# Stacking the halves of keys and queries by 96 transfers, not by TensorE

## The chip, the cores and the metric

The kernel runs on one NeuronCore of one Trainium2 chip. The metric is the device time of one execution in microseconds (us). The kernel before took 898.96 us, the median of three runs (898.91 to 900.83). The names of the engines: TensorE (PE, and PEld for its weight loads), VectorE (DVE), ScalarE (ACT), GpSimd (POOL) and SyncE (SP), which here only issues transfers.

## What is computed

A small vision tower of two layers over 32 images of 37 tokens (36 patches and a class token), 256 features wide: patch projection, a linear-recurrence attention, a quantized convolutional feed-forward, then a causal softmax attention and a mixture of 32 experts. The change lies in the second attention, of 16 heads of 16 features:

```python
q = jnp.einsum('bse,hde->bshd', x, Wq) + bq
k = jnp.einsum('bse,hde->bshd', x, Wk) + bk
v = jnp.einsum('bse,hde->bshd', x, Wv) + bv
mask = jnp.triu(jnp.full((s, s), -jnp.inf, dtype=x.dtype), k=1)
scores = (jnp.einsum('bqhd,bkhd->bhqk', q, k) + mask) * inv_scale
attn = jax.nn.softmax(scores, axis=-1)
out = jnp.einsum('bhqk,bkhd->bqhd', attn, v)
```

All is float32 in the reference. The kernel keeps each float32 operand of a product as two float16 halves, high and low, and multiplies high by high, high by low and low by high.

## The kernel before

Each engine has a program of its own, written out by hand; they meet at counting semaphores. `T` is 32 x 37 = 1,184 tokens, cut in `NCH` = 4 chunks of `CH` = 296. Features lie on the 128 partitions, in two groups `c` = 0, 1 of 128 features (8 heads each).

**Projection** (line 2037 on). TensorE computes for group 0 the keys (`i` = 1) and the queries (`i` = 0), chunk by chunk, then the values, then keys and queries of group 1. ScalarE writes the high half of each with its bias (L1252: `k1h`, `q1h`), VectorE the low half (L1692: `k1l`, `q1l`). The value halves (L1259, L1698) go to `vt`, and SyncE puts them on three groups of partition rows of `v3` by 18 transfers inside the core's memory (line 914 on; `load` is L887): three thirds, three residues of the sequence number, and 32 and 5 rows of each.

**Turning** (`turn_halves`, L2060 on). A score product contracts over 48 rows: 16 features of a head three times, as (high, high, low) of the queries against (high, low, high) of the keys. These rows must lie one above the other, and two heads lie in one stack, at rows 0 to 47 and 64 to 111. `PICK` says which half goes to which third. TensorE moves them there by products with 0/1 matrices (`picks`, made by GpSimd), 32 turns of four matmuls (L2069) of 296 columns, into two banks of its accumulator memory each; the turns go in turn to ScalarE (L488) and VectorE (L490), which copy 112 x 592 values to `qs` and `ks` as float16. 26 turns stand before the attention's loop, six in it, two in each of the first three units.

**Attention**, 16 units `k` of four sequences and eight heads; units 0 to 7 are group 0, 8 to 15 group 1. In program order TensorE issues in step `k`: the scores of unit `k` (L2085 puts the mask, L2094 the 32 score products), the turning of the probabilities of unit `k` - 3 (L2108), the mix of unit `k` - 4 (L2119 are four filling matmuls, L2127 the 32 products with `v3`). The first mix waits for the 18 transfers of `v3`. VectorE takes maximum and difference (L1706, L1710), ScalarE the exponential and the high half (L1273, L1277), GpSimd the low half (L1038), ScalarE and VectorE copy the turned probabilities (L1270, L1719), VectorE divides (L1724, L1725). In steps 7, 9, 11 and 13 ScalarE also makes the high half of an expert's weights, and in steps 9 and 11 VectorE a low half (L586); SyncE loads the next weights after each low half (L540). When the last unit is divided, the result is turned back (L2147), normalized and handed to the experts.

Of the kernel before, what the change touches and what calls it, by code (L numbers as in the profile page):

```python
# [13 lines left out]
DH = D // H  # L14
# [27 lines left out]
for _n, _w in [("cb", 6), ("cw", 24), ("gb", 2), ("dbb", 1), ("opb", 2), ("fcw", 24), ("fcb", 8), ("bq", 2),  # L42
# [32 lines left out]
    + ["pad1", "qk1h", "v1h", "v_one"]  # L75

    + ["v3", "turned", "turned_act", "turned_dve"]
# [136 lines left out]
TURNED = [(c, h, p, i) for c in range(2) for h in range(2) for p in range(4) for i in (1, 0)]  # L214
INSIDE = 6
FIRST_TURNS = len(TURNED) - INSIDE
TURN_LAG, MIX_LAG = 3, 4


def turner(t):  # L220
    return ("dve", "act")[(t // 2 + t) % 2]


def turn_bank(t):
    return 2 * (t % 4) if t < FIRST_TURNS else 4 + 2 * (t % 2)


def turn_holder(t):
    return max((x for x in range(t) if turn_bank(x) == turn_bank(t)), default=None)


def turned_inside(k):
    return range(FIRST_TURNS + 2 * k, FIRST_TURNS + 2 * k + 2) if 2 * k < INSIDE else ()


def turned_by(who, t):
    return sum(turner(x) == who for x in range(t + 1))
# [3 lines left out]
KK = 3 * DH  # L241

# [14 lines left out]
def tower(nc, a, out, probe=None):  # L257
    place = plan_tiles()
    order = list(place)
    with ExitStack() as ctx:  # L260
# [67 lines left out]
        def after(eng, key):  # L328

            eng.wait_ge(emptied[who(key)], nth(key))  # L330

        def cols(q, n=CH):
            return slice(q * n, (q + 1) * n)
# [108 lines left out]
        picks = carve(9344, 2, 2, 4, 64 + KK, dt=F16)  # L442
        v3 = carve(26272, B, H, DH + 1, dt=F16, parts=3 * S)
        o1 = carve(4608, BP, H, DH)
# [34 lines left out]

        def stack(eng, name, turns):  # L480
            for t in turns:
                c, h, p, i = TURNED[t]
                if turner(t) == name:
                    eng.wait_ge(ev["turned"], t + 1)
                    dst = (ks if i else qs)[:, 4 * c + p, 2 * CH * h:2 * CH * h + 2 * CH].rearrange("p (i t) -> p i t", i=2)
                    src = psum[0:64 + KK, turn_bank(t):turn_bank(t) + 2, 0:CH]
                    if name == "act":
                        eng.activation(dst, src, ACT.Copy).then_inc(ev["turned_act"], 1)  # L488
                    else:
                        eng.tensor_copy(dst, src).then_inc(ev["turned_dve"], 1)  # L490

        def stacked(eng, t):
            for name in ("act", "dve"):
                eng.wait_ge(ev["turned_" + name], turned_by(name, t))
# [390 lines left out]
        def _(sp):  # L885
            def load(dst, src, name):
                sp.dma_start(dst, src).then_inc(ev[name], 16)  # L887
# [23 lines left out]
            for e in range(2):  # L911
                load(wraw[:, e], a["wmoe"][0, e], f"wraw{e}")
            after(sp, ("v1", (VT + 1) // 2 - 1))
            for n, kind in enumerate((0, 1, 0)):
                for b in range(3):
                    m = (B - b + 2) // 3
                    for r, w in ((0, 32), (32, S - 32)):
                        load(v3[S * n + r:S * n + r + w, b:B:3].rearrange("p b h v -> p b (h v)"),
                             vt[S * b + r:S * b + r + w, kind, 0:m].rearrange("p n h v -> p n (h v)"), "v3")
            if not probe:  # L920
                moe_sp(sp)
# [7 lines left out]
        def _(pool):  # L929
# [96 lines left out]
            link(pool.memset(picks, 0.0))  # L1026
            for pattern in range(2):
                for n, kind in enumerate(PICK[pattern]):
                    for x in range(2):
                        ins = pool.tensor_copy(picks[:, pattern, kind, :, 64 * x + DH * n:64 * x + DH * n + DH],  # L1030
                                               identh[:].rearrange("p (i x d) -> p i x d", i=4, x=2)[:, :, x])
                        if (pattern, n, x) == (1, 2, 1):
                            ins.then_inc(ev["pad1"], 1)
                        else:
                            link(ins, hold=False)
# [7 lines left out]
        def _(act):  # L1043
# [218 lines left out]
            stack(act, "act", range(FIRST_TURNS))  # L1262
            for k in range(len(UNITS) + TURN_LAG):
                stack(act, "act", turned_inside(k))
                x = k - TURN_LAG
                if x >= 0:
                    act.wait_ge(ev["att_t"], 2 * x + 1)
                    if x >= 2:
                        act.wait_ge(ev["att_o"], x - 1)
                    act.activation(pt[0:3 * S, x % 2, 0:8], pt_bank(0), ACT.Copy).then_inc(ev["att_pa"], 1)  # L1270
                if k < len(UNITS):
                    act.wait_ge(ev["att_e"], k + 1)
                    act.activation(e_[0:101, k % 3], e_[0:101, k % 3], ACT.Exp, scale=DH ** -0.5).then_inc(ev["att_p"], 1)  # L1273
                    act.wait_ge(ev["att_p"], k + 1)
                    if k >= 3:
                        act.wait_ge(ev["att_t"], 2 * (k - 2))
# [10 lines left out]
        def _(dve):  # L1287
# [413 lines left out]
            stack(dve, "dve", range(FIRST_TURNS))  # L1701
            for k in range(len(UNITS) + MIX_LAG):
# [10 lines left out]
                stack(dve, "dve", turned_inside(k))  # L1713
# [39 lines left out]
        def _(pe):  # L1753
# [304 lines left out]
            halves = ((q1h, q1l), (k1h, k1l))  # L2058

            def turn_halves(t):  # L2060
                c, h, p, i = TURNED[t]
                if t == 0:
                    pe.wait_ge(ev["pad1"], 1)
                    after(pe, ("qk1", 0, 1, NCH - 1))
                if turn_holder(t) is not None:
                    stacked(pe, turn_holder(t))
                for x in range(2):
                    for kind in range(2):
                        ins = pe.matmul(psum[0:64 + KK, turn_bank(t) + x, 0:CH], picks[:, i, kind, p],  # L2069
                                        halves[i][kind][:, c, cols(2 * h + x)], start=kind == 0, stop=kind == 1)  # L2070
                ins.then_inc(ev["turned"], 1)

            for t in range(FIRST_TURNS):
                turn_halves(t)

            def scores(k):
                c, n = UNITS[k]
                if k < 2:
                    stacked(pe, max(t for t in range(FIRST_TURNS) if turn_bank(t) == 2 * k))
                elif n % 4 == 0:  # L2080
                    stacked(pe, 16 * c + 2 * n + 7)
# [17 lines left out]
            def turn_probs(k):  # L2099
                pe.wait_ge(ev["att_lo"], k + 1)  # L2100
                if k == 0:
                    stacked(pe, len(TURNED) - 1)
                else:
                    pe.wait_ge(ev["att_pa"], k)
                    pe.wait_ge(ev["att_pb"], k)
# [26 lines left out]
            for k in range(len(UNITS) + MIX_LAG):  # L2132
                if k < len(UNITS):
                    scores(k)
                for t in turned_inside(k):
                    turn_halves(t)
# [85 lines left out]
```

## Time and profile before

| | us |
|---|---|
| median of three runs | 898.96 |
| lowest and highest | 898.91, 900.83 |
| the profiled execution's own time | 899.29 |
| its span (first to last instruction) | 897.6 |
| TensorE busy | 762.5 |
| VectorE busy | 614.6 |
| ScalarE busy | 389.3 |
| GpSimd busy | 185.9 |

The profile is of one execution. Times of its rows count from the start of the span, so the execution's own time is the span and 1.7 us around it. An engine's busy time is the sum of its instructions; that of TensorE is modelled, since its matmuls overlap. "<-" in a row names what is written and what is read, with partitions x elements behind, and in brackets stands how long the engine had been idle and what ended it. Most of the kernel's data lies in one large buffer, `arena`, so many rows read "arena<-arena".

### The profile page before, as it was taken

How to read it: one execution, taken by the hardware profiler on the slowest of the kernel's cores; microseconds unless marked ns; L12 is line 12 of the kernel's file. 1: busy time of each engine (PE TensorE's matmuls, PEld its weight loads, DVE VectorE, ACT ScalarE, POOL GpSimd, SP SyncE). 2: the span in 40 equal slices, each digit the busy share in tenths (PEclk: the TensorE clock that was granted, in tenths of full speed). 3: DMA queues.
4: the chain of work that ended last, by engine and by line, in shares of the span. 5: the costliest groups of instructions: out<-in, count | busy, mean ns of one | idle time of the engine just before them, and what ended most of it. 6: DMA issues, size and time to landing. Idle time of an engine off the chain costs nothing.

```text
span 897.6 us, 19046 instructions
## 1 busy us (share of the span) xinstructions
PE 762.5 (85%) x7314; PEld 562.6 (63%) x7314; DVE 614.6 (68%) x974; ACT 389.3 (43%) x559; POOL 185.9 (21%) x197
## 2 busy tenths in 40 slices
PE   4786956989996966877598996699999999999997
PEld 3554735954543654656278884467777777777775
DVE  5796597658877476788767887757777755555554
ACT  5344653620224232765356983434444423333322
POOL 7000791005989801000300430000000000000000
PEclk9986877999999996987999998889999999999999
DMA  8000000020000000010112001044444312222221
GB/s 304 1 1 2 2 1 3 3 95 0 1 0 1 0 2 0 1 33 6 35 30 59 14 28 36 1 148 147 157 151 151 125 53 79 65 68 62 67 65 54
DMA packets 24070, 46.02 MB, mean 51 GB/s; under 512 B 2605, under 2 KB 10541, under 8 KB 23629
## 3 DMA queue, kind: packets, MB, share of 16 engines
q1 hardware_dynamic: 24013, 45.21, 16.5%
q8 instruction: 42, 0.69, 0.3%
q14 instruction: 15, 0.12, 0.0%
HBM read 41.91 MB, written 1.36 MB: 48 GB/s over the span
## 4 chain that ended last, share of the span: by engine, by line
PE 70%; DVE 18%; ACT 5%; issue 4%; POOL 1%; DMA 1%; SPq 0%; DVEq 0%; ACTq 0%; POOLq 0%
PE psum L1765 11%; PE psum L1766 11%; PE psum L1767 11%; PE psum L1941 6%; PE psum L1951 4%; PE psum L825 4%; PE psum L826 4%; PE psum L827 4%; PE psum L2069 1%; DVE arena L1445 1%; PE psum L1991 1%; PE psum L1922 1%; DVE arena L1638 1%; DVE arena L1310 1%; PE psum L2108 1%
## 5 line engine op out<-in xcount | busy, mean ns | idle before, releaser
L1765 PE MATMUL psum<-xh,arena 128*128 128x296 f16 (+1 forms) x664 | 196.4, 296 | 12.0 <-DVE xl L1318 6.3
L1766 PE MATMUL psum<-xl,arena 128*128 128x296 f16 (+1 forms) x664 | 196.3, 296 | 0.0
L1767 PE MATMUL psum<-xh,arena 128*128 128x296 f16 (+1 forms) x664 | 196.1, 295 | 0.0
L694 DVE TENSOR_TENSOR arena<-arena 128x592 f16<-128x592 f32 x68 | 52.7, 776 | 61.2 <-ACT arena L605 60.9
L600 ACT ACTIVATE arena<-psum 128x592 f32<-128x592 f32 x66 | 43.8, 664 | 115.3 <-PE psum L1767 115.3
L1765 PEld LDWEIGHTS psum<-xh,arena 128*128 (+2 forms) x664 | 66.2, 100 | 35.6 <-issue 9.4
L749 DVE TENSOR_TENSOR arena<-psum,arena 128x592 f32<-128x592 f32 x64 | 49.6, 775 | 50.9 <-PE psum L1767 50.2
L825 PE MATMUL psum<-arena 128*128 128x296 f16 x272 | 79.7, 293 | 4.6 <-DVE arena L694 3.8
L826 PE MATMUL psum<-arena 128*128 128x296 f16 x272 | 79.7, 293 | 0.0
L605 ACT ACTIVATE arena<-arena 128x592 f16<-128x592 f32 x66 | 46.0, 697 | 77.6 <-DVE arena L688 74.8
L827 PE MATMUL psum<-arena 128*128 128x296 f16 x272 | 79.6, 293 | 0.0
L1765 PE MATMUL psum<-arena 128*74 128x74 f16 (+3 forms) x348 | 59.2, 231 | 23.6 <-DVE arena L1328 12.7
L1767 PEld LDWEIGHTS psum<-xh,arena 128*128 (+2 forms) x664 | 66.3, 100 | 20.5
L1766 PEld LDWEIGHTS psum<-xl,arena 128*128 (+2 forms) x664 | 66.3, 100 | 19.6
L1941 PE MATMUL psum<-arena 128*128 128x512 f32 (+1 forms) x160 | 65.8, 550 | 14.3 <-DVE arena L524 14.3
L524 DVE TENSOR_TENSOR arena<-arena,psum 128x320 f32<-128x320 f32 (+7 forms) x67 | 54.1, 808 | 8.4 <-PE psum L1941 8.4
L1941 PEld LDWEIGHTS psum<-arena 128*128 128x128 f32 x160 | 30.3, 195 | 46.5 <-issue 28.4
L1007 POOL TENSOR_TENSOR arena<-arena 128x64 f32<-128x64 f32 (+23 forms) x24 | 43.7, 1819 | 75.8 <-ACT arena L1170 58.7
L1767 PE MATMUL psum<-arena 128*74 128x74 f16 (+3 forms) x348 | 59.2, 232 | 0.0
L1766 PE MATMUL psum<-arena 128*74 128x74 f16 (+3 forms) x348 | 59.2, 231 | 0.0
L688 DVE TENSOR_TENSOR arena<-arena 128x592 f32<-128x592 f32 x68 | 52.7, 776 | 8.8 <-ACT arena L600 1.9
L1765 PEld LDWEIGHTS psum<-arena 128*74 128x74 f16 (+2 forms) x348 | 38.8, 117 | 28.3 <-issue 24.6
(317 smaller groups left out, 1583.1 us busy)
## 6 DMA issues: line engine op xcount, KB each, us to landing
arena<-comb SPq DMA_DIRECT2D x62, 296.0 KB, 3.3
arena<-in_wmoe SPq DMA_DIRECT2D x34, 384.0 KB, 3.0
arena<-in_xt SPq DMA_DIRECT2D x4, 864.0 KB, 9.5
arena<-in_w SPq DMA_DIRECT2D x2, 1024.0 KB, 6.6
arena<-arena SPq DMA_DIRECT2D x6, 187.0 KB
arena<-in_ctrl SPq DMA_DIRECT2D x1, 1056.0 KB, 9.1
out<-arena SPq DMA_DIRECT2D x2, 512.0 KB, 3.1
arena<-in_wlin SPq DMA_DIRECT2D x1, 768.0 KB, 4.4
```

Of the source, the lines that this page charges most:

```text
L524: return eng.tensor_tensor(dst[:, 0:w * HJ * DH].rearrange("p (t j v) -> p t j v", j=HJ, v=DH), a_, u, ALU.mult)
L605: act.activation(ah[:, s_], t1, ACT.Copy).then_inc(ev["ah"], 1)
L688: dve.tensor_tensor(t1, t1, sg, ALU.mult).then_inc(ev["a"], 1)
L694: dve.tensor_tensor(al[:, s_], t1, ah[:, s_], ALU.subtract).then_inc(ev["al"], 1)
L749: dve.tensor_tensor(t1v, up, cb_[:, s_].rearrange("p (c t) -> p c t", c=2), ALU.mult).then_inc(ev["t1"], 1)
L825: pe.matmul(dst, high, ah[:, s_, cols(ch)], start=start, stop=False, skip_group_check=True)
L826: pe.matmul(dst, high, al[:, s_, cols(ch)], start=False, stop=False, skip_group_check=True)
L827: ins = pe.matmul(dst, low, ah[:, s_, cols(ch)], start=False, stop=stop, skip_group_check=True)
L1765: pe.matmul(dst, wh, mh, start=start, stop=False)
L1766: pe.matmul(dst, wh, ml, start=False, stop=False)
L1767: return pe.matmul(dst, wl, mh, start=False, stop=stop)
L1941: pe.matmul(row(g0, g1 - g0), negident, ring[:, n_ % RING, 64 * (g0 - base):64 * (g1 - base)], start=False, stop=s_ + 1 == g0, skip_group_ ...
```

## The change

The turning products and their copies are gone, with the 0/1 matrices and the functions that ordered them. SyncE issues a transfer for each head, group and third in their place: 8 heads x 3 thirds x (keys, queries) x 2 groups = 96, each of 16 partitions by 1,184 float16 values (2,368 bytes), from the place where the half was written to its rows of `qs` or `ks`. For each group and kind, 16 (the thirds with the high half) wait for ScalarE's four high halves, and 8 for VectorE's last low half. TensorE waits for 48 landed transfers before unit 0 and for the other 48 before unit 8. The buffer `o1` of the results is moved, since the halves are now read longer.

```diff
@@ SyncE's program
+            halves = ((q1h, q1l), (k1h, k1l))
+
+            def stack(c, i):
+                sp.wait_ge(ev["qk1h"], NCH * (2 * c + 2 - i))
+                for part in range(2):
+                    if part:
+                        after(sp, ("qk1", i, c, NCH - 1))
+                    for n, kind in enumerate(PICK[i]):
+                        for h in range(8 if kind == part else 0):
+                            row = 64 * (h % 2) + DH * n
+                            load((qs, ks)[i][row:row + DH, 4 * c + h // 2],
+                                 halves[i][kind][DH * h:DH * h + DH, c], f"stacked{c}")
+
+            stack(0, 1)
+            stack(0, 0)
             after(sp, ("v1", (VT + 1) // 2 - 1))
             for n, kind in enumerate((0, 1, 0)):
...
+            stack(1, 1)
+            stack(1, 0)
             if not probe:
                 moe_sp(sp)
@@ TensorE's program
-            for t in range(FIRST_TURNS):
-                turn_halves(t)
-
             def scores(k):
                 c, n = UNITS[k]
-                if k < 2:
-                    stacked(pe, max(t for t in range(FIRST_TURNS) if turn_bank(t) == 2 * k))
-                elif n % 4 == 0:
-                    stacked(pe, 16 * c + 2 * n + 7)
+                if n == 0:
+                    pe.wait_ge(ev[f"stacked{c}"], 16 * STACKS)
+                if k == 0:
+                    after(pe, ("qk1", 0, 1, NCH - 1))
...
                 pe.wait_ge(ev["att_lo"], k + 1)
-                if k == 0:
-                    stacked(pe, len(TURNED) - 1)
-                else:
+                if k:
                     pe.wait_ge(ev["att_pa"], k)
                     pe.wait_ge(ev["att_pb"], k)
...
-                for t in turned_inside(k):
-                    turn_halves(t)
@@ VectorE's program (ScalarE's alike)
-            stack(dve, "dve", range(FIRST_TURNS))
...
-                stack(dve, "dve", turned_inside(k))
@@ GpSimd's program
-            link(pool.memset(picks, 0.0))
-            for pattern in range(2):
...
@@ buffers
-        o1 = carve(4608, BP, H, DH)
+        o1 = carve(21536, BP, H, DH)
```

SyncE's queue before, from the first expert weights to the first transfers of the values and from their last to the next weights (L887 is `load`, in_wmoe are expert weights, arena<-arena is a transfer inside the core's memory; sizes are partitions x runs x values):

```order
L887 DMA arena<-in_wmoe 128x768 [waits emptied_f2]
L887 DMA arena<-in_wmoe 128x768
L887 DMA arena<-arena 32x11x272 [waits emptied_dve]
L887 DMA arena<-arena 5x11x272
...
L887 DMA arena<-arena 32x10x272
L887 DMA arena<-arena 5x10x272
L540 DMA arena<-in_wmoe 128x768 [waits wlo] x4
```

The same place with the change (`load` is now L848, the weights' L501):

```order
L848 DMA arena<-in_wmoe 128x768 [waits emptied_f2]
L848 DMA arena<-in_wmoe 128x768
L848 DMA arena<-arena 16x1184 [waits qk1h]
L848 DMA arena<-arena 16x1184 x15
L848 DMA arena<-arena 16x1184 [waits emptied_dve]
L848 DMA arena<-arena 16x1184 x7
...
L848 DMA arena<-arena 32x11x272 [waits emptied_dve]
L848 DMA arena<-arena 5x11x272
...
L848 DMA arena<-arena 16x1184 [waits emptied_dve]
L848 DMA arena<-arena 16x1184 x7
L501 DMA arena<-in_wmoe 128x768 [waits wlo] x4
```

48 of the new transfers stand ahead of the 18 of the values, and 48 behind them.

TensorE's queue before, between the last projection and the scores of unit 0 (L1767 is a projection product, L2069 a turning product, L2085 and L2094 the scores):

```order
L1767 MATMUL psum<-xh,arena 128x296
L2069 MATMUL psum<-arena 112x296 [waits emptied_dve,pad1]
L2069 MATMUL psum<-arena 112x296 x15
L2069 MATMUL psum<-arena 112x296 [waits turned_dve,turned_act]
L2069 MATMUL psum<-arena 112x296 x3
...
L2085 MATMUL psum<-arena 101x296 [waits turned_dve,turned_act]
L2085 MATMUL psum<-arena 101x296
L2094 MATMUL psum<-arena 64x37 x8
```

And with the change (L1731 the projection, L2031 and L2040 the scores, L2052 the turned probabilities, L2063 the filling of the first mix):

```order
L1731 MATMUL psum<-xh,arena 128x296
L2031 MATMUL psum<-arena 101x296 [waits emptied_dve,stacked0]
L2031 MATMUL psum<-arena 101x296
L2040 MATMUL psum<-arena 64x37 x8
...
L2052 MATMUL psum<-identh,arena 111x101 [waits att_pb,att_pa,att_lo]
L2052 MATMUL psum<-identh,arena 111x101 x15
L2063 MATMUL psum<-arena 101x222 [waits v3]
...
L2031 MATMUL psum<-arena 101x296 [waits att_e,stacked1]
```

The scores now follow the projection directly, with a wait on `stacked0`; a wait on `stacked1` stands before the scores of unit 8.

## Rows read from the trace of the kernel before

**Rows 1.** The page, busy time of each engine (share of the span) and instructions.
```profile
PE 762.5 (85%) x7314; PEld 562.6 (63%) x7314; DVE 614.6 (68%) x974; ACT 389.3 (43%) x559; POOL 185.9 (21%) x197
```

**Rows 2.** Chain of waits, 470 to 486 us: start, us, what.
```profile
470.64 0.54 DVE arena L1692
...
471.31 12.27 PE psum L2069 x96
...
483.61 1.47 DVE arena L490 x2
```

**Rows 3.** Instructions of the turning's lines: ns min/median/max, first and last start.
```profile
L2069 PE MATMUL psum<-arena x128: 289/289/333, 471.3 to 491.6; 128*112 128x296 f16 x128
...
L490 DVE CAST arena<-psum x16: 764/765/776, 472.0 to 492.0; 112x592 f16<-112x592 f32 x16
...
L488 ACT ACTIVATE arena<-psum x16: 639/661/665, 472.5 to 492.9; 112x592 f16<-112x592 f32 x16
```

**Rows 4.** Time line of SyncE's issues: start, us, instruction, count.
```profile
9.84 0.45 SPq L887 DMA_DIRECT2D arena<-in_ctrl  x1
...
12.30 0.43 SPq L887 DMA_DIRECT2D arena<-in_wout  x1
...
465.09 13.93 SPq L887 DMA_DIRECT2D arena<-arena  x18
...
466.85 0.65 SPq L887 DMA_DIRECT2D arena<-arena  x1
...
467.54 0.78 SPq L887 DMA_DIRECT2D arena<-arena  x1
...
514.10 6.41 SPq L540 DMA_DIRECT2D arena<-in_wmoe  x2
```

**Rows 5.** Issues in the experts' loop; landing of the store from 32 partitions.
```profile
L543 SPq DMA_DIRECT2D arena<-comb x62: 332/333/371, 585.8 to 878.4; - x62
...
comb<-arena SPq DMA_DIRECT2D x1, 148.0 KB, 2.0
```

**Rows 6.** DMA, 582 to 585 (store), 747 to 751 (load): packets, MB, share.
```profile
q1 hardware_dynamic: 48, 0.15, 22.2%
...
q1 hardware_dynamic: 144, 0.30, 22.2%
```

**Rows 7.** Time line, TensorE and VectorE, 485 to 540 us: scores, mix, division.
```profile
485.21 0.43 PE L2085 MATMUL psum<-arena 101*101 101x296 bf16 x2 [0.63 <-DVE arena L490]
...
496.99 0.56 PE L2119 MATMUL psum<-arena 101*101 101x222 bf16 x4
...
503.87 0.46 PE L2085 MATMUL psum<-arena 101*101 101x296 bf16 x2
...
506.71 0.46 PE L2085 MATMUL psum<-arena 101*101 101x296 bf16 x2
...
527.17 0.46 PE L2085 MATMUL psum<-arena 101*101 101x296 bf16 x2
...
538.66 0.42 DVE L1725 TENSOR_TENSOR arena<-psum,arena 101x256 f32<-101x256 f32 x1
```

**Rows 8.** Time line, ScalarE and VectorE: key, query and value halves.
```profile
453.84 0.51 ACT L1252 ACTIVATE arena<-psum,small 128x296 f16<-128x296 f32 x1 [0.56 <-PE psum L1767]
...
457.40 0.53 DVE L1692 SCALAR_TENSOR_TENSOR arena<-psum,small,arena 128x296 f16<-128x296 f32 x1 [0.23 <-ACT arena L1252]
...
464.04 1.02 DVE L1698 TENSOR_TENSOR arena<-psum,arena 111x512 f16<-111x512 f32 x2 [0.61 <-ACT arena L1259]
```

**Rows 9.** Busy time and granted clock (PEclk) in stretches from 443 to 456 us.
```profile
core 0: us, PE busy (x) PEld busy (x) DVE busy (x) ACT busy (x) POOL busy (x), PEclk, DMA share, GB/s
443.00:448.00 5.00, 0.78 (x8) 0.31 (x8) 4.07 (x5) 1.38 (x2) 4.21 (x14) 0.84 0.00 0
448.00:453.00 5.00, 4.87 (x20) 2.87 (x21) 4.41 (x8) 2.54 (x5) 0.00 (x0) 0.50 0.00 0
453.00:456.00 3.00, 3.00 (x24) 2.30 (x23) 1.69 (x4) 1.80 (x4) 0.00 (x0) 0.96 0.00 0
```

More of the change, by code:

```diff
@@ L73 @@
     + ["wsum", "wq", "xabs", "am1", "mx1_tok", "xq", "fy", "fconv", "sil", "fabs", "am2", "mx2_tok", "scaled", "hq", "hqa", "wnorm", "wround", "mxpad", "taps"]
-    + ["pad1", "qk1h", "v1h", "v_one"]
-    + ["v3", "turned", "turned_act", "turned_dve"]
+    + ["qk1h", "v1h", "v_one"]
+    + ["v3", "stacked0", "stacked1"]
     + ["att_s", "att_max", "att_e", "att_p", "att_hi", "att_lo", "att_t", "att_pa", "att_pb", "att_o", "att_n"]
@@ L213 @@
 PICK = ((0, 0, 1), (0, 1, 0))
-TURNED = [(c, h, p, i) for c in range(2) for h in range(2) for p in range(4) for i in (1, 0)]
-INSIDE = 6
-FIRST_TURNS = len(TURNED) - INSIDE
 TURN_LAG, MIX_LAG = 3, 4
[L220 to L237, printed above, removed]
 UNITS = [(c, n) for c in range(2) for n in range(BP // 2)]
 KK = 3 * DH
+STACKS = 48
 PROBE = {"s1": ("op", 1, NCH - 1), "s2": ("f2", 1, NCH - 1), "s3": ("OT", 7)}
@@ L441, in tower @@
         ks = carve(16800, 8, T, dt=F16, parts=64 + KK)
-        picks = carve(9344, 2, 2, 4, 64 + KK, dt=F16)
         v3 = carve(26272, B, H, DH + 1, dt=F16, parts=3 * S)
-        o1 = carve(4608, BP, H, DH)
+        o1 = carve(21536, BP, H, DH)
         vt = carve(30624, 2, VT, H, DH + 1, dt=F16, parts=3 * S)
@@ L478, in tower @@
         PT_BANK, O_BANK = 4, 6
[L480 to L488, printed above, removed]
-                    else:
[L490 to L494, printed above, removed]
         def s_banks(k):
@@ L1025, in _ @@
             pool.memset(vt[:, 1], 0.0).then_inc(ev["v_one"], 1)
-            link(pool.memset(picks, 0.0))
-            for pattern in range(2):
[L1028 to L1035, printed above, removed]
             for k in range(len(UNITS)):
@@ L1261, in _ @@
                                        ACT.Copy).then_inc(ev["v1h"], 1)
-            stack(act, "act", range(FIRST_TURNS))
             for k in range(len(UNITS) + TURN_LAG):
-                stack(act, "act", turned_inside(k))
                 x = k - TURN_LAG
@@ L2057, in _ @@
                         ins.then_inc(filled[who(("v1", n))], 1)
[L2058 to L2071, printed above, removed]
-            for t in range(FIRST_TURNS):
-                turn_halves(t)
             def scores(k):
                 c, n = UNITS[k]
-                if k < 2:
-                    stacked(pe, max(t for t in range(FIRST_TURNS) if turn_bank(t) == 2 * k))
-                elif n % 4 == 0:
-                    stacked(pe, 16 * c + 2 * n + 7)
+                if n == 0:
+                    pe.wait_ge(ev[f"stacked{c}"], 16 * STACKS)
+                if k == 0:
+                    after(pe, ("qk1", 0, 1, NCH - 1))
                 if k >= 2:
@@ L2100, in turn_probs @@
                 pe.wait_ge(ev["att_lo"], k + 1)
-                if k == 0:
-                    stacked(pe, len(TURNED) - 1)
-                else:
+                if k:
                     pe.wait_ge(ev["att_pa"], k)
```

## The prediction

> **What bounds the kernel now.** I read the page first, then the chain of waits around the change, the instruction rows of the lines that go, SyncE's issues, and last the time line of the attention loop. TensorE is busy 85% of the span and the other engines less [rows 1], but the change touches one stage only, so that stage decides. Its chain has nothing but TensorE's turning in it: it starts 0.1 us after VectorE has written the last low half (470.64 + 0.54) and runs 12.27 us without a gap; then come the last two casts of VectorE, 1.47 us [rows 2]. The first score products follow at 485.21 [rows 7]. From there a unit (four sequences, eight heads) takes TensorE 506.71 - 503.87 = 2.84 us, and the last result of unit 15 is written at 538.66 + 0.42 = 539.1 [rows 7]. SyncE meanwhile issues only the 18 transfers of the values, in 13.93 us, and then nothing until 514.10 [rows 4].
>
> **What goes.** 128 turning matmuls of 289 ns (overlapped; the chain prices 96 of them at 12.27 us), 16 casts of VectorE at 0.765 us and 16 copies of ScalarE at 0.661 us [rows 3]. On the path that is 485.21 - 471.2 = 14.0 us ahead of unit 0. The casts and copies of the last six turns stand between the units 0 to 2 and are no longer on any path, since something later holds the first mix (below). GpSimd's 13 small instructions and the wait on them cost nothing: GpSimd is long done. The output buffer's new place costs nothing.
>
> **What comes.** 96 transfers of 16 partitions by 2,368 bytes (37.9 KB), all on SyncE's one queue, 48 for each half of the heads. TensorE waits for the first 48 before unit 0, and for the second 48 before unit 8. In the queue the order is: 48 transfers, the 18 of the values, 48 transfers. So three things are now in a line that were not: the values wait for 48 issues, the second half waits for 66, and what SyncE loads after it (expert weights) for 114.
>
> The price of one issue decides everything. No row shows a transfer of 16 partitions. The nearest are plain transfers of one run per partition, issued one behind the other from 128 partitions: six start from 9.84 to 12.30 (the first and the last are shown), five steps in 2.46 us, 0.492 us each [rows 4]. An issue inside the experts' loop shows 0.333 us [rows 5]; with the 0.04 us between issues that is 0.375, the low side. The 18 value transfers (two-dimensional, half of them of 5 partitions) take 13.93/18 = 0.774 us each [rows 4], the high side. I take 0.492, the row with the same form in the same situation.
>
> The data must not be slower than that. A store from 32 partitions moves 32 packets of 4.7 KB in 22.2% of 16 engines for 3 us, 10.7 us in all, 0.33 us a packet; a load to 128 partitions moves 128 of 2.4 KB in 22.2% of 4 us, 14.2 us, 0.11 us each [rows 6]. Per byte the store from few partitions is 1.5 times as slow. With 16 partitions I allow it twice the store's time per byte: 0.33 us per packet of 2.4 KB, 16 of them side by side, so 0.33 us per transfer, under the 0.492 of the issue. Landing is 2.0 us after the start of an issue, as for the store [rows 5].
>
> The Trainium skill, SBUF — State Buffer, Door 1: The DMA port swizzle, has a rule that bears on this: bandwidth follows how many of 16 ports the partitions reach, and partitions 0 to 15 reach four, measured there at 104 GB/s. By it a transfer takes 37.9/104 = 0.36 us (an estimate from that page), 96 of them 35 us in place of the 47 of the sum; the trace's slower store from 32 partitions agrees in direction [rows 6]. If the ports and not the issue set the pace, the time would be that of the second rival at most; it also speaks against any hope that small transfers go out much faster than 0.33 us.
>
> The sum, along SyncE's queue:
> - ScalarE ends the fourth high half of the keys at 453.84 + 0.51 = 454.35; a SyncE wait ended 0.03 us after its releaser before (465.09 against 464.04 + 1.02) [rows 4, 8]. Start 454.4. It doesn't wait again: it reaches the keys' low halves at 454.4 + 16 x 0.492 = 462.3, and VectorE has written all of the first group at 457.40 + 0.53 = 457.9 [rows 8]; the values are written at 465.1, the second group at 471.2, both before their turn.
> - 48 x 0.492 = 23.6: issued at 478.0, landed at 477.5 + 2.0 = 479.5. Unit 0 starts there, 5.7 us earlier than before. This gain doesn't last:
> - the values' 18 issues, 13.95 us: 478.0 to 492.0 [rows 4]. Landed 2.0 us after the last one's start (491.2), by 493.4 with 0.2 for their larger size. The first mix, at 496.99 before [rows 7], comes at 493.4. TensorE, which runs in order, has units 5 and on queued behind that mix; units 0 to 4 need some 8 us from 479.5, so it stands still about 5 us. From the first mix to unit 8 there were 506.71 - 496.99 = 9.7 us: TensorE asks for unit 8 at 503.1.
> - second half: 48 issues from 492.0 to 515.6, landed at 515.1 + 2.0 = 517.1. TensorE stands still from 503 to 517, with turn 5 and mix 4 queued behind the scores of unit 8, and VectorE, ScalarE and GpSimd run dry behind it.
> - so unit 8 starts 517.1 - 506.7 = 10.4 us later than before. From unit 8 to the end there were 539.1 - 506.7 = 32.4 us. Two corrections: VectorE and ScalarE start with nothing left over, and the 7 steps to unit 15 took 527.17 - 506.71 = 20.5 us where TensorE alone needs 7 x 2.84 = 19.9: minus 0.6. And after an idle time the granted clock is low: 0.50 in the 5 us from 448, after TensorE had done 0.78 us of work in 5, and 0.96 in the next 3 us [rows 9]. 5 us at half clock lose up to 2.5 us of TensorE's work; transposes and mixes are not all bound by columns, so 2.0.
> - 10.4 + 2.0 - 0.6 = +11.8 us. What follows the attention starts later and is otherwise the same; the expert weights 2 and 3 wait for VectorE's events of units 9 and 11, which come after SyncE is free (before at 514.10, free now at 515.6 with those units shifted by 12) and stay hidden.
>
> The profiled execution took 899.29 us (span 897.6 and 1.7 around it), 0.3 above the median of 898.96. 899.3 + 11.8 = 911.1, and by the median 910.8: I say 911. A change of under 0.2% (1.8 us, 897.2 to 900.8) can't be told from none.
>
> **Rival 1: an issue costs less with fewer rows, faster than before.** Mechanism: SyncE's time for an issue has a part per partition, and 16 in place of 128 save it. Unit 8 starts at 454.4 + 96p + 13.95 + 1.6 (p the step), and with the 1.4 for clock and drained engines it is faster than before by over 1.8 us when 96p is under 33.5, p under 0.35. With p = 0.30: unit 8 at 498.8, asked for at about 494, so 7.9 us earlier, less 1.4: 893. For it: the 0.333 us row [rows 5]. Against it: that one has 128 partitions too, so it speaks for the place of an issue and not for its rows; the value transfers go from 32 and from 5 partitions in turn, and the third (32) took 0.65 us, the fourth (5) 0.78 [rows 4], so fewer rows don't make an issue shorter there; and the data bound of 0.33 us stands just under the limit. Chance 0.06.
>
> **Rival 2: the step is 0.375 us.** Issues then end at 454.4 + 36.0 + 13.95 = 504.4, landed 506.0, 0.7 before unit 8's old start; with 1.4 it is +0.7 us, 900: no change. TensorE's 14 us are used up by SyncE's queue exactly. For and against as above. Chance 0.07.
>
> **Rival 3: an issue costs as much as the values' or the ports hold reads and writes of the same few partitions apart.** Source and target both lie in memory rows of the core, and both in 16 partitions; if reading and writing don't overlap, 2 x 0.33 = 0.66 us per transfer; if issues go like the 18, 0.774. The first gives 96 x 0.66 = 63.4: unit 8 at 533.4, +26.7 + 1.4 = +28, 927; the second 74.3: +39, 938. Speaking for it: the value transfers, also within the core's memory, are the only ones of that kind in the trace and are the slow ones. Against: they are two-dimensional (11 runs in each partition) and differ in that from the 96. Chance 0.13.
>
> The forecast, step of 0.43 to 0.56 us, gives 905 to 917 (96 x 0.06 = 6 us to each side, a little more above) and has 0.74.
>
> **How the numbers follow.** Faster: rival 1 and a sliver of the fast end, 0.07. Same: 0.07. Slower: the rest, 0.86. The range takes in the forecast's own, half of the distance to rival 2 and half of that to rival 3: 902 to 924.
>
> **What would show it.** SyncE's 96 issues with a step near 0.49 us; no turning on TensorE; its idle time before unit 0 (470 to 479.5) put down to these transfers; a second idle time of about 5 us before the first mix, put down to the values, and a third of about 14 us before unit 8, the only one that counts. A granted clock of 0.5 after it for some 5 us. The step wrong shows as a multiple of 96 in the place of unit 8. The prediction is wrong in kind if unit 8 doesn't wait, or if the step is right and the end moves by less than 6 us.

## The result, and the profile after

The changed kernel takes 944.91 us (943.39 to 947.07, 4 runs), the kernel before 899.89 on the same chip: ratio 1.050, 95% interval [1.047, 1.053]. The direction was forecast, the size was not: 911 with a range of 902 to 924. The profiled execution took 945.82 us, span 944.1, which is 46.5 more than before.

The page, busy time of each engine, beside [rows 1]:

```profile
PE 781.3 (83%) x7186; PEld 574.0 (61%) x7186; DVE 607.3 (64%) x958; ACT 380.7 (40%) x543; POOL 182.2 (19%) x184
```

TensorE runs 128 instructions less and is busy 19 us longer. That is the first sign that something else than a wait was added.

SyncE's issues on the time line (start, us, instruction, count) and the same line's instructions (ns min/median/max, first and last start), beside [rows 4]:

```profile
453.43 77.45 SPq L848 DMA_DIRECT2D arena<-arena  x114
```
```profile
L848 SPq DMA_DIRECT2D arena<-arena x114: 573/589/1881, 453.4 to 530.3; - x114
```

The start is 1.0 us before the forecast one (454.4). An issue takes 589 ns, with the 44 between two issues 0.633 us a step, not 0.492. The maximum of 1,881 ns is one of three long issues. This piece of the time line, and the queues of the same 3 us, show one:

```profile
503.68 3.78 SPq L848 DMA_DIRECT2D arena<-arena  x5
```
```profile
q1 hardware_dynamic: 114, 0.14, 21.2%
q8 instruction: 1, 0.02, 2.1%
```

Five issues take 3.78 us here in place of 3.1, and a packet of the instruction queue falls into it; the other two (3.87 and 4.41 us for five) have one too. Together they cost 2.7 us: 77.45 less 96 x 0.633 and less the values' 13.95. (Two more such packets fell among the values' issues, at 488.87 and 493.77; behind the first SyncE paused 0.4 us, the second lengthened nothing.)

TensorE and VectorE on the time line, beside [rows 7] (L2031 scores, L2063 the filling before the mix, L1689 division):

```profile
486.05 0.73 PE L2031 MATMUL psum<-arena 101*101 101x296 bf16 x2 [16.93 <-DMA arena<-arena]
...
501.11 0.98 PE L2063 MATMUL psum<-arena 101*101 101x222 bf16 x4 [3.96 <-DMA arena<-arena]
...
532.37 0.73 PE L2031 MATMUL psum<-arena 101*101 101x296 bf16 x2 [15.30 <-DMA arena<-arena]
...
537.02 0.73 PE L2031 MATMUL psum<-arena 101*101 101x296 bf16 x2
...
564.91 0.73 PE L2031 MATMUL psum<-arena 101*101 101x296 bf16 x2
```
```profile
582.22 0.42 DVE L1689 TENSOR_TENSOR arena<-psum,arena 101x256 f32<-101x256 f32 x1
```

The three waits on transfers are where they were forecast. But a unit takes 537.02 - 532.37 = 4.65 us in place of 2.84, and the same two products 0.73 in place of 0.46. Busy time and granted clock (PEclk) by stretches say why, beside [rows 9]:

```profile
456.00:472.00 16.00, 13.12 (x113) 11.51 (x111) 8.75 (x16) 9.14 (x16) 0.00 (x0) 1.00 0.26 58
472.00:486.00 14.00, 0.00 (x0) 0.00 (x0) 0.00 (x0) 0.00 (x0) 0.00 (x0) 0.53 0.27 59
486.00:502.00 16.00, 10.42 (x206) 7.42 (x206) 8.68 (x12) 10.49 (x12) 6.33 (x5) 0.50 0.64 132
502.00:516.00 14.00, 14.00 (x260) 11.63 (x260) 8.44 (x15) 6.77 (x8) 2.52 (x2) 0.50 0.25 54
516.00:532.00 16.00, 1.07 (x33) 0.97 (x32) 0.68 (x2) 1.98 (x3) 1.26 (x1) 0.50 0.27 60
532.00:588.00 56.00, 54.82 (x904) 46.44 (x905) 32.73 (x62) 27.73 (x32) 10.10 (x8) 0.50 0.06 16
588.00:600.00 12.00, 8.55 (x51) 4.84 (x49) 9.06 (x16) 3.29 (x5) 0.00 (x0) 0.93 0.21 67
```

The clock falls to its lower level (1.2 GHz of 2.4) in the first idle time and stays there to the end of the loop. From 532 to 588 us TensorE is busy 54.82 of 56 us and still gets 0.50. In the kernel before the same loop fills the engine as much, at 1.00:

```profile
507.00:520.00 13.00, 12.84 (x396) 10.92 (x395) 12.47 (x24) 12.84 (x16) 5.09 (x4) 1.00 0.12 35
```

| us | before | forecast | after |
|---|---|---|---|
| unit 0 | 485.2 | 479.5 | 486.1 |
| first mix | 497.0 | 493.4 | 501.1 |
| unit 8 | 506.7 | 517.1 | 532.4 |
| unit 8 to the last result | 32.4 | 33.8 | 50.3 |
| last result to the end of the span | 358.5 | 358.5 | 361.5 |

The 46.5 us are 25.7 (unit 8 later), 17.9 (the loop behind it) and 2.9 (behind the loop), of which the forecast had 10.4, 1.4 and 0.

### The profile page after: what moved, and what is told of

The parts are those of the page before. It is cut to its first block, busy times and chain, and to the rows that moved or that the text cites. A ratio compares the mean times of both kernels' runs of the same rounds, so it can differ in the third digit from the quotient of the medians.

```text
span 944.1 us, 18808 instructions
## 1 busy us (share of the span) xinstructions
PE 781.3 (83%) x7186; PEld 574.0 (61%) x7186; DVE 607.3 (64%) x958; ACT 380.7 (40%) x543; POOL 182.2 (19%) x184
## 4 chain that ended last, share of the span: by engine, by line
PE 69%; DVE 15%; SPq 6%; ACT 4%; issue 4%; POOL 1%; DMA 1%; DVEq 0%; ACTq 0%; POOLq 0%
PE psum L1729 11%; PE psum L1730 11%; PE psum L1731 11%; SPq L848 6%; PE psum L1905 6%; PE psum L1915 4%; PE psum L786 4%; PE psum L787 4%; PE psum L788 4%; PE psum L2052 2%; DVE arena L1411 1%; PE psum L2071 1%; PE psum L1955 1%; PE psum L1886 1%; PE psum L2063 1%
## 5 line engine op out<-in xcount | busy, mean ns | idle before, releaser
L1731 PE MATMUL psum<-xh,arena 128*128 128x296 f16 (+1 forms) x664 | 197.7, 298 | 0.0
L1731 PEld LDWEIGHTS psum<-xh,arena 128*128 (+2 forms) x664 | 66.9, 101 | 21.2
L1905 PE MATMUL psum<-arena 128*128 128x512 f32 (+1 forms) x160 | 65.8, 550 | 13.5 <-DVE arena L485 13.5
L1731 PE MATMUL psum<-arena 128*74 128x74 f16 (+3 forms) x348 | 59.0, 232 | 0.0
```

Of the source, the lines that this page charges most:

```text
L1731: return pe.matmul(dst, wl, mh, start=False, stop=stop)
L1905: pe.matmul(row(g0, g1 - g0), negident, ring[:, n_ % RING, 64 * (g0 - base):64 * (g1 - base)], start=False, stop=s_ + 1 == g0, skip_group_ ...
```

## Experiments

Times are medians; "before" is the kernel before on the same chip. The runs differ by up to 4 us in where SyncE's first of these transfers starts (453.4 to 457.1), so that lengths inside the loop tell more than times on the axis.

**What an issue costs.** The kernel before, with nine series of ten transfers behind its end (128 to 16 partitions, 2,368 or 128 bytes from each, out of DRAM or out of the core's memory); PN is 10:

```diff
+            probes = [
+                (0, 128, 592, a["xt"][:, 0, 0:592]),
+                (0, 128, 592, pa[:]),
+                (0, 32, 592, pa[32:64]),
+                (0, 16, 592, pa[16:32]),
...
+                for n in range(PN):
+                    load(pb[r:r + rows, n, 0:w], src, "probe")
```

> The kernel before, with 9 series of 10 transfers behind its last store, each series awaited: (1) from DRAM to 128 partitions, 2368 bytes each; (2) memory to memory inside the core, 128 partitions; (3) the same with 32; (4) with 16 partitions; (5) 16 partitions of 128 bytes; (6) DRAM to 16 partitions; (7) 16 partitions, 64 to 79; (8) DRAM to 128 partitions of 128 bytes; (9) 64 partitions inside the core. Their time adds to the kernel's and is no matter. Theory A (source inside the core makes the issue slower): series 2, 3, 4, 5, 7, 9 show 0.63 us from start to start, 1, 6 and 8 show 0.48. Theory B (few partitions make it slower): 4 to 7 show 0.63, and 1, 2, 8 show 0.48. Theory C (data holds the queue): 5 is faster than 4.

Four of the series on SyncE's time line: from the core's memory on 128 partitions, from DRAM to 16 partitions, from the core's memory on 16 partitions, from DRAM to 128 partitions with 128 bytes each:

```profile
910.62 6.83 SPq L888 DMA_DIRECT2D arena<-arena  x10
...
942.68 4.50 SPq L888 DMA_DIRECT2D arena<-in_xt  x10
948.64 6.20 SPq L888 DMA_DIRECT2D arena<-arena  x10
956.28 4.62 SPq L888 DMA_DIRECT2D arena<-in_xt  x10
```

Over a series, a step from the core's memory is 0.62 to 0.68 us, a step from DRAM 0.45 to 0.47 in the two series shown, one of 16 partitions and one of 128. With 16 partitions from the core's memory it is 0.63 us for 2,368 bytes and for 128. So for transfers as small as these neither rows nor bytes set the price; the kind of source does, which is theory A. Only the large series (64 or 128 partitions of 2,368 bytes) lengthen towards their end, to 0.70 to 0.78 us a step from the core's memory and 0.63 and 0.75 from DRAM: there the size shows. The 0.492 of [rows 4] were loads from DRAM, the wrong neighbour.

**The clock, by filling the waits.** The changed kernel with filler products (101x222, results unused): 145 before unit 0, 55 before the first mix, 215 before unit 8.

```diff
+                if k == 8:
+                    pe.wait_ge(ev["att_n"], 3)
+                    warm_up(0, WARM[1])
```

> The changed kernel with filling matmuls of 222 columns ahead of three waits of TensorE: 145 before unit 0, 55 before the first mix, 215 before unit 8. They fill idle time and compute nothing that is used. Theory (clock): in the changed kernel the granted clock stayed at 0.50 from 473 to 589 us, and the loop's step grew from 2.84 to 4.65 us; with TensorE busy during the waits the clock stays at 1.0, unit 8 starts at the same place (532 us, SyncE sets it), a step is 2.84 us, the last unit ends near 564 in place of 582, and the 3 us lost behind the loop come back too: 944.9 - 18 - 3 = 924 us. Rival (pipeline): VectorE, ScalarE and GpSimd run dry during the wait and it is their refilling that makes the steps long; then fillers change nothing and the time stays within 3 us of 945.

927.92 us (4 runs), ratio to before 1.031 [1.028, 1.034].

```profile
515.00:525.00 10.00, 10.00 (x106) 10.00 (x104) 0.50 (x2) 2.08 (x3) 1.27 (x1) 1.00 0.23 50
...
536.00:550.00 14.00, 13.84 (x430) 11.79 (x428) 12.97 (x24) 12.20 (x15) 4.63 (x4) 1.00 0.10 32
```

Unit 8 starts at 535.71, the last result comes 32.3 us later, as before (32.4), not 50.3. The engines had run dry in that wait as they do in the changed kernel, and no step is long for it: so the 17.9 us of the loop behind unit 8 are the clock's. (In the first half the clock fell here too, at about 487, in a wait of 2.15 us that was left before unit 0, and was back at about 501, in the 55 fillers.) With the 215 alone (one run, 936.03) it is the same: units 0 to 7 at 0.50, unit 8 at 542.99, since the fillers themselves began slowly and ended late, and again 32.3 us from there.

> The changed kernel with filler products in front of unit 8 alone (215 of 101x222, the idle time in which TensorE waits for the second 48 transfers), none before unit 0 and the first mix. Theory (the second half of the loop is slow only for the clock that the idle time left low, and wide products in that idle time bring it back): clock 0.5 in units 0 to 7 as in the changed kernel, 1.0 from unit 8, steps 2.84: about 928, as with fillers at all three places. Rival (the clock is lost for good in the first idle time, before unit 0, and fillers later don't bring it back): steps of 4.65 in the second half, and the fillers themselves at half rate end late: 960 or more.

**Is the wait before unit 8 needed for the loss?** First the 24 transfers of group 1's queries left out (its scores read group 0's queries), then the second 48 issued by GpSimd:

```diff
-            stack(1, 0)
...
-                                            qs[rows, 4 * c + h // 2, t0:t0 + m], ks[rows, 4 * c + h // 2, t0:t0 + S],
+                                            qs[rows, h // 2, t0:t0 + m], ks[rows, 4 * c + h // 2, t0:t0 + S],
```

> The changed kernel with 24 transfers fewer: the queries of the second group of heads aren't stacked, and the scores of that group take the first group's queries in their place. All else is the same. Theory (SyncE's queue): an issue takes 0.633 us from start to start, so unit 8 starts 24 x 0.633 = 15.2 us earlier, near 517, and with the clock still low the time falls by 15 us to 930. Rival (data): if the landing and not the issue holds the queue, the saving per transfer is not 0.633 but what the data takes; the waits would then end at another place than the last issue plus 2 us.

```diff
-            stack(1, 1)
-            stack(1, 0)
...
+            stack_by(pool, 1, 1)
+            stack_by(pool, 1, 0)
```

> The changed kernel with the second group's 48 transfers issued by GpSimd, which is idle there, and not by SyncE. Theory (one queue's issue time is the limit): the queues run side by side, GpSimd starts its 48 at 471 when the second group's halves are written; if its issue takes about 1 us, unit 8 can start near 521, and if it takes 0.6, near 502; TensorE asks for it at 516 at the low clock. GpSimd's low half of unit 0 (needed by the first turned probabilities) is queued behind the 48, so at 1 us an issue the loop's first units wait until about 519: time 930 to 940. At 0.6 us: unit 8 not late at all, time 925 to 930. Rival (all transfers share what limits them): an issue or its data gets slower on both queues and the time stays at 945.

931.9 (2 runs) and 931.76 us (ratio 1.034 [1.032, 1.037]). In neither does unit 8 wait. GpSimd's issues, and two of the stretches of the second:

```profile
469.56 23.17 POOL L855 DMA_DIRECT2D arena<-arena  x48 [24.45 <-ACT arena L1221]
```
```profile
515.00:525.00 10.00, 10.00 (x196) 8.40 (x192) 5.70 (x11) 6.77 (x8) 2.54 (x2) 0.50 0.02 3
525.00:536.00 11.00, 11.00 (x213) 8.97 (x213) 8.16 (x14) 6.26 (x8) 3.08 (x3) 0.50 0.12 37
```

GpSimd's step is 23.17/48 = 0.483 us, less than SyncE's, and SyncE's went on beside it. The Trainium skill, DMA: Bandwidth & Descriptors, Rules for kernel authors, says that spreading transfers over engines only saves issue time; that is what was short here. Yet 13 us of the 45 come back and no more: the loop runs at 0.50 from its start to its end, without the second wait.

**Wide products inside the loop.** The changed kernel with FILLERS 12 in place of 4, so that every unit has 12 fillers before its mix:

> The changed kernel with 12 filler products (101x222) in front of each mix in place of 4, 16 units x 8 = 128 more; nothing else. TensorE is busy all through the loop in both. Theory A (what keeps the low clock is that the loop's products are short; more wide columns per step bring it back): the clock rises to 1.0 within the first units after unit 0 or at the latest after unit 8; the first-half loop is then no longer than the wait for the transfers, and the second half has steps of about 2.84 + 8 x 0.095 = 3.6 us: 16 us shorter or so for it, less 6 for the fillers: about 935. Theory B (the low clock lasts whatever TensorE is given): steps of 4.65 + 8 x 0.19 = 6.2 us, 945 + 8 x 1.5 + 3 = about 960.

966.52 us (one run), clock 0.50 through the whole loop, near theory B's 960: theory A falls. Twelve wide products in each slow unit don't bring the clock back; 215 in a row do.

**Better arrangements of the transfers.** All 96 kept but split over SyncE (24 keys, values, 16) and GpSimd (24, 24 and 8 inside units 0 to 3), with a few fillers; and half of the change, group 1 by transfers and group 0 by TensorE:

```diff
+            stack_by(pool, 0, 0, tail="p")
+            stack_by(pool, 1, 1, tail="p")
...
+                if k < 4:
+                    stack_by(pool, 1, 0, parts=(1,), heads_=(2 * k, 2 * k + 1), tail="p")
```

> The whole change kept (96 transfers, no turning products), but its issues split over two engines in the order in which they are wanted: SyncE takes the 24 of group 0's keys, the 18 of the values and the 16 high ones of group 1's queries; GpSimd takes the 24 of group 0's queries, the 24 of group 1's keys and, two heads a unit in units 0 to 3, the 8 low ones of group 1's queries. Small filler products (8 before unit 0, 6 to 12 before units 1 to 4, the first mix and unit 8) are put in where TensorE stood. Theory (issues cost 0.633 us on SyncE and 0.483 on GpSimd, and the clock stays up if TensorE hardly stands): unit 0 at about 454 + 24 x 0.633 + 2 = 471, values landed at 469 + 14 + 2 = 485, first mix there, unit 8 not waited for; the loop ends some 11 us before that of the kernel before: about 889. Rival (a stand of a few us in front of unit 0 is enough for the clock to stay low through the loop): steps of the loop 4.65 us in place of 2.84, 15 x 1.8 = 27 more: about 916. Rival (the two queues slow each other): unit 0 not before 477, about 897.

```diff
-TURNED = [(c, h, p, i) for c in range(2) for h in range(2) for p in range(4) for i in (1, 0)]
-INSIDE = 6
+TURNED = [(c, h, p, i) for c in range(1) for h in range(2) for p in range(4) for i in (1, 0)]
+INSIDE = 0
```

> Half of the change, on the kernel before: TensorE turns group 0 alone (16 turns, none inside the loop), group 1's keys come by 24 transfers that GpSimd issues after the selection matrices, and its queries by 24 that SyncE issues after the values; unit 8 waits for both. Theory: 10 turns less in front of unit 0 and 6 less in the loop, both series of transfers (24 x 0.63 = 15 us on SyncE, 24 x 0.48 = 12 us on GpSimd) are done before unit 8, and TensorE doesn't stand, so that the clock stays at 1.0: faster by 5 to 9 us, about 892. Rival (the first mix is held by the values, not by the turns, and what is saved in front is given back there): same, 898 to 900. Rival (GpSimd's issues run into the loop and delay the third parts of the probabilities, or the gap before the loop lets the clock fall): slower, 905 or more.

926.35 (1.031 [1.028, 1.034]) and 918.72 us (1.022 [1.020, 1.025]): both missed. In the half version TensorE never stood longer than 1.0 us after unit 0 began, and the clock was at 0.50 in the whole window from 486 us. What was missing there too are the six turns among units 0 to 2. In the split version two waits on TensorE's time line say what was missed:

```profile
484.32 1.74 PE L2065 MATMUL psum<-identh,arena 101*111 101x101 f16 x16 [5.22 <-POOL arena L1007]
...
496.21 0.98 PE L2077 MATMUL psum<-arena 101*101 101x222 bf16 x4 [3.75 <-DMA arena<-arena]
```

GpSimd's low half of unit 0 stood behind its 48 issues (459.87 to 482.98), and in that wait of 5.22 us the clock fell. The values, issued by 487.0, then held the first mix until 496.2, with the DMA engines 95% busy from 470 to 486 us. So both versions met the low clock, which their rivals had named, but at waits inside the loop.

**The turns inside the loop.** The kernel before with INSIDE 0: all 32 turns ahead of unit 0, no transfer added, nothing left out.

> The kernel before with all of its 32 turns in front of unit 0 and none inside the loop: the same products and copies, no transfer added. Theory W (the clock of the loop hangs on the wide products among units 0 to 2): granted clock 0.5 within some us of unit 0 and through most of the loop, steps of 4.65 in place of 2.84 us: 899 + 3 (six turns of 0.5 us earlier in the queue) + about 22 = about 920 to 925. Rival T (the low clock comes from the transfers or from the long idle time before the loop, neither of which is here): clock 1.0, about 900 to 902.

927.3 us, ratio 1.029 [1.027, 1.032]. Stretches of that kernel:

```profile
486.00:490.00 4.00, 4.00 (x81) 3.53 (x83) 2.89 (x5) 3.19 (x5) 0.00 (x0) 1.00 0.01 4
490.00:494.00 4.00, 2.33 (x100) 1.38 (x85) 3.90 (x6) 3.13 (x5) 0.78 (x1) 0.78 0.00 0
494.00:498.00 4.00, 3.18 (x57) 2.68 (x56) 2.81 (x5) 3.97 (x5) 2.91 (x3) 0.50 0.02 4
```

Theory W came true, at 927 where it had put 920 to 925: moving six turns by some us costs 26 us. The change removes these turns along with the others, so it might have met the low clock even with transfers that cost nothing; no run shows that.

**Which gap?** The half version with its last six turns inside units 0 to 2 (INSIDE 6, GpSimd and SyncE sharing the 48); then that without its transfers (group 1 reads group 0's rows); then the first again with 64 fillers between the front turns and unit 0; then the first again with 10 fillers behind the scores of units 3 and 4, which wait for the last turn's copy (`stacked(pe, 15)`):

> Half of the change, with the loop fed as in the kernel before: TensorE turns group 0 alone (16 turns), 10 of them in front of unit 0 and the last 6 inside units 0 to 2, where the kernel before has its last 6 too. Group 1's keys (24) and, two a unit in units 0 to 3, the low halves of its queries (8) are issued by GpSimd, the 16 high ones by SyncE after the values. Theory W (the clock falls where the loop starts with narrow products and short waits alone, and 8 products of 296 columns a unit in units 0 to 2 keep it up): clock 1.0 through the loop; unit 0 some 3 us before the 481.1 of the half version without turns inside, 478; the first mix at 489 to 490, unit 8 at 500, which makes 6 us less than before: about 893. Rival T (the transfers themselves bring the clock down, or delay the values): clock 0.5 from 487 on as without the turns inside, about 917.

> The half version with turns inside the loop, without its 48 transfers: the scores of group 1 read the rows of group 0 (that much of the computation is left out). Everything that TensorE does up to unit 8 is as there. Theory T (the transfers' traffic brings the clock down): clock 1.0 through the loop, no wait before unit 8: about 891. Theory W (TensorE's own work does: the wide products ahead of the loop last 5.2 us in place of 13.3, then come short gaps): the clock falls at about 489 us as with the transfers, steps of 4.65 us, about 915.

> The half version with turns inside the loop and its 48 transfers, with 64 filler products (101x222, 0.095 us each, 6.1 us) between the last front turn and unit 0, so that the stretch of wide products ahead of the loop is as long as in the kernel before and unit 0 comes at about 485. Theory W (the work ahead of the gaps decides): clock 1.0 through the loop, the end as in the kernel before: 897 to 901. Theory T (the transfers decide): the clock falls in the first units all the same: about 922.

```diff
+                if k in (3, 4):
+                    stacked(pe, 15)
+                    warm_up(10)
```

> The half version with turns inside the loop and its 48 transfers, with 10 filler products (0.95 us) behind the scores of units 3 and 4, where TensorE stood 1.0 and 0.9 us and the clock fell. Theory W in its narrow form (the gaps in units 3 and 4 decide): clock 1.0 through the loop, unit 8 at 500 us, about 893: faster than the kernel before. If the stretch ahead or the transfers decide instead, the clock falls as without them: about 918.

917.43 (ratio 1.018 [1.015, 1.020]), 916.5 (one run), 922.86 (1.026 [1.024, 1.028]) and 894.11 us (0.993 [0.991, 0.996]). Transfers are not the cause (the second has none beside the values'), nor is the length of the wide stretch ahead (the third). Twenty fillers at the right place are enough. Without them (first kernel), and with them (last kernel):

```profile
487.03 1.00 PE L2126 MATMUL psum<-identh,arena 101*111 101x101 f16 x16 [1.02 <-ACT arena L488]
487.87 0.42 PE L2103 MATMUL psum<-arena 101*101 101x296 bf16 x2
489.57 1.71 PE L2126 MATMUL psum<-identh,arena 101*111 101x101 f16 x16 [0.92 <-ACT arena L1287]
```
```profile
487.57 1.18 PE L2093 MATMUL psum<-arena 101*101 101x222 bf16 x10 [1.04 <-ACT arena L488]
489.41 0.42 PE L2108 MATMUL psum<-arena 101*101 101x296 bf16 x2
490.13 1.18 PE L2093 MATMUL psum<-arena 101*101 101x222 bf16 x10
491.14 0.99 PE L2134 MATMUL psum<-identh,arena 101*111 101x101 f16 x16
493.18 0.46 PE L2108 MATMUL psum<-arena 101*101 101x296 bf16 x2
496.02 0.46 PE L2108 MATMUL psum<-arena 101*101 101x296 bf16 x2
```
```profile
533.64 0.42 DVE L1742 TENSOR_TENSOR arena<-psum,arena 101x256 f32<-101x256 f32 x1
```

In the first the turned probabilities go from 1.00 to 1.71 us within one unit. In the last the wait in unit 3 is still there (1.04 us) and the fillers come behind it; only the wait in unit 4 (0.92) is filled. So what kept the clock is not that no gap is left. Whether one of the two groups of fillers would do, no run shows. The loop keeps 2.84 us a unit and the last result comes at 534.1, 5.0 us before that of the kernel before. This version is the only one that beats the kernel before, by 0.7%: 894.1 against 899.4.

**Fillers behind the first units in the changed kernel,** 12 behind the scores of units 0 to 3, beside those of the first filler experiment:

> The changed kernel with filler products at the three places of the first filler experiment and 12 more of 101x222 behind the scores of each of units 0 to 3. Theory W: the granted clock of 486 to 502 us, 0.57 there, is now 0.9 or more, and the loop's first half runs at 2.8 us a unit; the end hangs on the second 48 transfers, so that the time falls only a little: 922 to 928. Rival (the fall at about 487 us comes whatever TensorE does): clock 0.5 to 0.6 there as before, time about 930.

935.91 us (one run), a miss: the clock fell at about 490 all the same, after a wait of 1.39 us for the transfers before unit 0, and the fillers then ran at half rate and took time themselves. TensorE was busy all of the time from 490 to 510 us, a good part of it with wide products, and got 0.50.

**What stays open.** The kernel before has the same gaps and keeps its clock:

```profile
490.70 1.20 PE L2069 MATMUL psum<-arena 128*112 128x296 f16 x8 [0.87 <-DVE arena L490]
...
493.60 1.00 PE L2108 MATMUL psum<-identh,arena 101*111 101x101 f16 x16 [1.08 <-ACT arena L488]
...
496.15 1.00 PE L2108 MATMUL psum<-identh,arena 101*111 101x101 f16 x16 [0.92 <-ACT arena L1270]
```

The version with 64 front fillers has these rows 3.22 us earlier with the same waits (0.87, 1.08, 0.92), and its clock falls at the last of them, whose products take 1.22 us in place of 1.00. It differs ahead of unit 0 in 64 fillers of 222 columns where the kernel before has turns of 296, in a wait of 0.63 us before unit 0 that only the kernel before has, and in its transfers. So the kernel before is likely close to losing its clock; which of these keeps it, or whether it is where in time the gaps fall, no run shows. In each of its runs beside these experiments it did keep it: they took 896.97 to 902.32 us, with a mean granted clock of 0.922 to 0.935, where the two half versions first shown have 0.888 to 0.899.

## Why the prediction was wrong

- **What bounds the stage, and that three waits come** held. The waits stood where they were named: 16.9 us before unit 0, 4.0 before the first mix, 15.3 before unit 8. That the last is so near the forecast's 14 is luck: TensorE asked for unit 8 at 517.1 and not 503.1, and the transfers landed 15.3 us later.
- **The gain of 5.7 us before unit 0** was none: 48 issues, one of them long, took 31.2 and not 23.6.
- **The issue step failed.** "I take 0.492, the row with the same form in the same situation" took loads from DRAM; the row that was nearest in the source's place, the values' 0.774, was put into rival 3 with a chance of 0.13. The 0.333 that spoke for rivals 1 and 2 [rows 5] has its source in DRAM too. The measured 0.633 lies between. It moves unit 8 by 96 x 0.141 = 13.5 us, long issues add 2.7, the start gives back 1.0: 15.2 of the 15.3 us between forecast (517.1) and trace (532.4). Rival 3's place for unit 8, 533.4, was nearly right by luck, its 927 was not, and the mechanism that gave this place (reading and writing the same few partitions apart, 0.66 us) is not what the runs show: an issue of 16 partitions takes the same 0.63 us with 128 bytes as with 2,368, and unit 8 starts 2.1 us after the start of the last issue.
- **The port bound** of the Trainium skill (SBUF — State Buffer, Door 1: The DMA port swizzle) couldn't decide: the estimate from it, 0.36 us a transfer, is below the issue of 0.633.
- **The clock term failed, and more than its size.** "5 us at half clock lose up to 2.5 us" assumed from [rows 9] that work brings the clock back within some us. That row is of projection products of 296 columns each, one behind the other. The loop's short products with TensorE busy did not bring it back in 56 us. Term forecast: 2.0; measured: 17.9 in the loop behind unit 8. The -0.6 for the drained engines was nothing: with the clock at 1.00 and the engines as dry, the same stretch took 32.3 us against 32.4. The 2.9 us behind the loop are not explained: that stretch took 357.0 to 361.5 us in these runs, 358.5 in the kernel before, and the clock is low in places there in all of them. The Trainium skill, TensorE: Matmul & The Clock Gate, What's actually happening, says that a throttled clock is the default and activity releases it; the trace agrees for the 215 fillers in a row (0.50 before them, 1.00 behind them), and not for the loop, where 98% busy stayed at 0.50; what was measured decides.
- **"The casts and copies of the last six turns ... are no longer on any path"** missed what the turns did beside their work. The kernel before with them moved ahead of the loop takes 26 us more, with no transfer added. In the changed kernel itself the clock fell earlier, in the wait before unit 0, and the half version with six turns in their place lost it all the same, so these turns alone don't decide.
- **Sum:** 11.8 forecast + 15.3 (queue) + 16.5 (clock in the loop) + 2.9 = 46.5.

Had the step been known exactly, the forecast would have been 926 and still 19 us short. The rival that wasn't on the list is that the clock, once down, stays down for the loop.

## What to carry to other kernels

Before you take work from TensorE, ask what its clock will do: in this loop of short products the clock fell at waits of about 1 us (in the half version, 917 us) and stayed low while the engine read fully busy, and two groups of wide fillers of 1.2 us each, at and behind these waits, were worth 23 us. Where they stand decides: 64 ahead of the loop, or 12 in each unit once the clock was down, brought nothing. Price a DMA issue from a row with the same source memory, not the same shape, and multiply by the count: 96 issues on one queue are a serial program. Moving half of the work, over two queues, with these fillers, won 5 us where moving all of it lost 45.

## What the runs showed of the hardware

- SyncE's issue step hangs on the source: 0.62 to 0.68 us from the core's memory, 0.45 to 0.47 from DRAM, for 16 or 128 partitions (but for the longer last steps of the large series). GpSimd's step for the 16-partition transfers is 0.483 us.
- A packet of the instruction queue beside an issue of the 96 goes with 0.7 to 1.3 us more for that issue (three times in the changed kernel; in the run with fillers at all three waits six times of six). Beside the values' issues it did not.
- TensorE's clock stayed at 0.50 through 56 us with the engine 98% busy with short products, while the same half of the loop entered at 1.00 kept 1.00 (kernel before, and the versions with 215 fillers before unit 8).
- TensorE's clock fell in the loop where the engine had stood no longer than 1.1 us at a time (half version with turns inside: waits of 0.86, 1.02 and 0.92 us).
